# A two-layer graph network on one core: edge keys formed by another engine, copies reordered at a seam, and a branch set elsewhere

## The reference

```
h = relu(layernorm(x))
# layer 0: two graph convolutions; S(h)[d] = sum of h[s] over edges (s, d)
h = relu(relu((h + S(h)) W1 + b1) W2 + b2)
x = x + relu((h + S(h)) W3 + b3) W4 + b4
h = relu(layernorm(x))
# layer 1: message passing
y = mlp3(h; WM, bM)            # per edge source, the same for all edges of a node
x = x + mlp3([h, S(y)]; WU, bU)
```

## Time and profile before

| | |
|---|---|
| median of 3 runs | 923.52 us (922.7 to 924.86) |
| the profiled execution | 923.8 us |
| its span, first to last instruction | 921.9 us |
| PE busy | 862.5 us (94%) |
| DVE busy | 697.5 us (76%) |
| ACT busy | 479.4 us (52%) |
| POOL busy | 395.4 us (43%) |
| DMA | 126.85 MB, mean 138 GB/s |

### The profile page before, as it was taken

One profiled execution on the slowest core, in us unless ns is written; L12 is line 12 of the kernel. 1 busy time (PEld: TensorE's weight loads), 2 busy tenths in 40 slices (PEclk: granted clock), 3 DMA queues, 4 the chain that ended last, 5 costly groups with the idle time before them and its releaser, 6 DMA issues.

```text
span 921.9 us, 25227 instructions
## 1 busy us (share of the span) xinstructions
PE 862.5 (94%) x11291; PEld 710.6 (77%) x11291; DVE 697.5 (76%) x658; ACT 479.4 (52%) x573; POOL 395.4 (43%) x281
## 2 busy tenths in 40 slices
PE   0588999999899999899999999999999999999998
PEld 0367898999898999678877777777778866777776
DVE  7879999999999997385545656654565676787785
ACT  2753646655444454274545555454545555555543
POOL 5888888888000000307645566410110143444532
PEclk9989899999999999999999999999999999999999
DMA  3025255444443244405444344434433567888873
GB/s 112 19 88 156 85 156 157 132 139 130 143 143 122 95 143 143 136 23 160 119 140 121 104 129 127 127 99 134 121 99 86 150 196 204 229 237 244 230 218 107
DMA packets 81856, 126.85 MB, mean 138 GB/s; under 512 B 10160, under 2 KB 58544, under 8 KB 81616
## 3 DMA queue, kind: packets, MB, share of 16 engines
q1 hardware_dynamic: 78608, 121.98, 44.0%
q0 software_dynamic: 3136, 3.22, 1.7%
HBM read 84.22 MB, written 40.94 MB: 136 GB/s over the span
## 4 chain that ended last, share of the span: by engine, by line
PE 55%; ACT 1%; DVE 1%; issue 1%; POOL 0%; POOLq 0%; DVEq 0%; ACTq 0%
PE net_ps_hi L1343 15%; PE net_ps_lo L1343 15%; PE net_ps_lo L1360 7%; PE net_ps_hi L1360 7%; PE net_ps_mt L1288 5%; PE net_ps_ft L1288 2%; PE net_ps_check L1378 1%; PE net_ps_hi L1288 1%; PE net_ps_lo L1288 1%; ACT net_wide L1171 1%; PE net_ps_mt L1390 1%; DVE net_wide L867 1%; PE net_ps_mt L1430 0%; ACT net_hid L1174 0%; PE net_ps_ft L1297 0%
## 5 line engine op out<-in xcount | busy, mean ns | idle before, releaser
L1343 PE MATMUL net_ps_hi<-net_wide,net_first 128*128 128x512 f32 (+2 forms) x637 | 246.7, 390 | 0.0
L1343 PE MATMUL net_ps_lo<-net_wide,net_first 128*128 128x512 f32 (+2 forms) x637 | 238.8, 378 | 0.0
L867 DVE CAST net_wide<-net_raw 128x3584 fp32r<-128x3584 uint8 (+2 forms) x90 | 206.9, 2306 | 41.8 <-PE net_ps_lo L1360 15.8
L1171 ACT ACTIVATE net_wide<-net_raw 128x3584 fp32r<-128x3584 uint8 (+2 forms) x64 | 193.6, 3025 | 79.1 <-PE net_ps_lo L1343 46.3
L607 PE MATMUL build_ps_out<-build_parts_pad,build_cnts 128*128 128x195 bf16 x2401 | 226.7, 254 | 1.0 <-ACT build_cnts L474 1.0
L345 DVE TENSOR_TENSOR build_hot_lo<-build_grid_lo,build_keys_t 128x4096 bf16<-128x4096 bf16 x98 | 220.4, 2281 | 0.0
L607 PEld LDWEIGHTS build_ps_out<-build_parts_pad,build_cnts 128*128 128x128 fp8e4 x2401 | 206.8, 100 | 5.3 <-ACT build_cnts L474 1.1
L474 ACT ACTIVATE build_cnts<-build_ps_cnt 128x980 uint16<-128x980 f32 (+2 forms) x173 | 148.9, 912 | 117.8 <-PE build_ps_cnt L587 115.4
L1343 PEld LDWEIGHTS net_ps_hi<-net_wide,net_first 128*128 128x128 f32 x637 | 119.7, 188 | 28.0 <-issue 7.5
L1343 PEld LDWEIGHTS net_ps_lo<-net_wide,net_first 128*128 128x128 f32 x637 | 119.9, 188 | 23.0 <-issue 2.6
L867 POOL CAST net_wide<-net_raw 128x3584 fp32r<-128x3584 uint8 (+2 forms) x28 | 84.8, 3030 | 109.7 <-PE net_ps_hi L1360 53.1
(11 more groups left out here) (192 smaller groups left out, 712.1 us busy)
## 6 DMA issues: line engine op xcount, KB each, us to landing
net_raw<-edge_counts SPq DMA_DIRECT2D x154, 448.0 KB, 3.7
edge_counts<-build_cnts SPq DMA_DIRECT2D x168, 224.0 KB
net_raw<-edge_counts SPq DMA_DIRECT2D x14, 336.0 KB, 3.3
net_raw<-edge_counts SPq DMA_DIRECT2D x14, 224.0 KB, 2.6
xres<-in_x SPq DMA_DIRECT2D x1, 1568.0 KB, 7.1
out<-xres SPq DMA_DIRECT2D x11, 128.0 KB, 4.2
build_rows<-in_dst_rows,build_row_i POOLq DMA_INDIRECT x49, 3.9
build_edges<-in_edges,build_start_i POOLq DMA_INDIRECT x49, 3.4
```

The source lines that it names most:

```text
L867: return issue(expanded[e % WIDE_RING][:, 0:n, :, :].rearrange("p w a d -> p (w a d)"), raw[e % RAW_RING][:, 0:n, :, :].rearrange("p w a d ...
L1171: expand(act, lambda to, x: nc.scalar.activation(to, x, ACT.Identity), e).then_inc(grown["act"], 1)
L1343: last = nc.tensor.matmul(ps[(b + 1) % 2][:, 0:n * P], first[:, c, lo:lo + H], expanded[e % WIDE_RING][:, 0:n, k, :], start=(c == 0), stop ...
```

## The change

- `find_keys` is gone from VectorE. ScalarE makes four 16-bit planes per pair straight from the gathered edges (`take_bytes`: three instructions of 128 elements; `take_distances`: two of 64), behind its copies of steps 0 and 1 of the pair two ahead of use. TensorE combines them while turning: four products (256, 128, 128, 128 columns) in place of two transposes of 128. The factor 64 is put back by `copy_keys`.
- All groups have 4 windows (the first 2, the last 3). Rows of a group are gathered one group ahead of its edges; from the seventh group on (g >= 6) its rows are compared six pairs ahead and the starts are written five pairs ahead.
- In the written-out beginning, keys of pair 1 are turned and copied right after the first four count steps, those of pair 2 after six.
- The use of pair 0 waits for the features' third parts piece by piece.
- At the seam, ScalarE makes the copy of the high part of y for the last three blocks (`upper_y`), VectorE splits block 12 before it expands its next piece, and ScalarE expands its piece before `upper(11)`.
- SyncE reads the flag and branches two stores earlier; its last two stores and the wait for all stores stand behind the branch.
- The check reads the edges and not the keys.

The core of the diff (line numbers in its headers left out):

```
-SPANS = [(0, 2), (2, 6), (6, 10), (10, 14), (14, 18)] + [(w, min(w + 2 * STEP, NW)) for w in range(18, NW, 2 * STEP)]
+SPANS = [(0, 2)] + [(w, min(w + STEP, NW)) for w in range(2, NW, STEP)]
-ROWS_BEHIND = {2: (4,), 3: (5,), 5: (6, 7), 6: (8,)}
...
-    return {4: (1, 2), 5: (3, 0)}.get(g, (FIRST_PAIR[g] - 6 - 2 * (g - 6), 0))
+    return {4: (2, 1), 5: (4, 1)}.get(g, (FIRST_PAIR[g] - 6, 1))
...
-    return {3: (1, 1), 4: (2, 1), 5: (4, 1)}.get(g, (FIRST_PAIR[g] - 5 - 2 * (g - 6), 1))
+    return {3: (1, 3), 4: (3, 1), 5: (5, 1)}.get(g, (FIRST_PAIR[g] - 5, 1))
...
                 for g in range(2, len(SPANS)):
                     gather_edges(g, *SPANS[g])
-                    for later in ROWS_BEHIND.get(g, ()):
-                        gather_rows(later, *SPANS[later])
+                    if g + 2 < len(SPANS):
+                        gather_rows(g + 2, *SPANS[g + 2])
...
-                def find_keys(g):
-                    lo, hi = SPANS[g]
-                    n = hi - lo
-                    dve.wait_ge(edges_in[g], 16 * n)
-                    src, dst = edges[:, lo:hi, :, 0], edges[:, lo:hi, :, 1]
-                    link(v.tensor_scalar(tile_no[:, 0:n, :], src, 7, None, ALU.logical_shift_right))
-                    v.scalar_tensor_tensor(keys[:, 0, lo:hi, :], tile_no[:, 0:n, :], float(-P), src, ALU.mult, ALU.add)
-                    link(v.scalar_tensor_tensor(scaled[:, 0:n, :], dst, 64.0, tile_no[:, 0:n, :], ALU.mult, ALU.add))
-                    last = v.tensor_tensor(keys[:, 1, lo:hi, :], scaled[:, 0:n, :],
-                                           node64[:, lo:hi, None].broadcast_to([P, n, RUN]), ALU.subtract)
...
+                def take_bytes(u):
+                    g = group_of(u)
+                    to = key_bytes[:, u % BYTE_RING, :, :].rearrange("p k (w e) -> p k w e", e=RUN)
+                    source = edges[:, 2 * u:2 * u + both(u), :, :].bitcast(U8).broadcast_to([P, 2, RUN, 4])
+                    act.wait_ge(edges_in[g], 16 * (SPANS[g][1] - SPANS[g][0]))
+                    nc.scalar.activation(to[:, 0, :, :], source[:, :, :, 0], ACT.Identity, scale=1 / 64)
+                    nc.scalar.activation(to[:, 1, :, :], source[:, :, :, 1], ACT.Identity, scale=-4.0)
+                    nc.scalar.activation(to[:, 2, :, :], source[:, :, :, 0], ACT.Sign, bias=cut[:, 0:1])
+
+                def take_distances(u):
+                    to = key_bytes[:, u % BYTE_RING, 3, :].rearrange("p (w e) -> p w e", e=RUN)
+                    for t in range(2):
+                        w = min(2 * u + t, NW - 1)
+                        last = nc.scalar.activation(to[:, t, :], edges[:, w, :, 1], ACT.Identity, bias=node128[:, w:w + 1],
+                                                    scale=float(-P))
+                    last.then_inc(keyed, 1)
...
                         copy_counts(u, k)
+                        if 0 < u < NU - 2 and k == 0:
+                            take_bytes(u + 2)
+                        if 0 < u < NU - 2 and k == 1:
+                            take_distances(u + 2)
...
                 def turn_keys(u, to):
-                    pe.wait_ge(keyed, group_of(u) + 1)
-                    for k in range(2):
-                        last = nc.tensor.transpose(to[:, k, :], keys[:, k, 2 * u:2 * u + 2, :].rearrange("p w e -> p (w e)"),
-                                                   ident_b[:, :])
-                    return last
+                    pe.wait_ge(keyed, u + 1)
+                    low, tile, top, away = (key_bytes[:, u % BYTE_RING, i, :] for i in range(4))
+                    nc.tensor.matmul(to, top, minus_b[:, None, :].broadcast_to([P, 2, P]), start=True, stop=False)
+                    nc.tensor.matmul(to[:, 0, :], low, ident_b[:, :], start=False, stop=False)
+                    nc.tensor.matmul(to[:, 1, :], tile, ident_b[:, :], start=False, stop=False)
+                    return nc.tensor.matmul(to[:, 1, :], away, ident_b[:, :], start=False, stop=True)
...
+                    if BLOCKS - 1 in at("ty", p - 1):
+                        split_y(BLOCKS - 1)
                     if p + AHEAD < 2 * LATER and EXPAND[p + AHEAD][0] == "dve":
                         grow(p + AHEAD)
...
+                def upper_y(b):
+                    w, n = windows(b), size(b)
+                    act.wait_ge(y_high, b + 1)
+                    nc.scalar.activation(by_turn(second[:, w, 0:F], b), turned_view(high_f, b), ACT.Identity).then_inc(y_upper, 1)
...
-                flagged = flag(sp)
-                for b in range(BLOCKS - 4, BLOCKS):
+                for b in range(BLOCKS - 4, BLOCKS - 2):
                     store(sp, b)
-                general_sync(sp, flagged, stored, 16 * BLOCKS)
-                sp.wait_ge(stored, 16 * BLOCKS)
+                def last_stores():
+                    for b in range(BLOCKS - 2, BLOCKS):
+                        store(sp, b)
+                    sp.wait_ge(stored, 16 * BLOCKS)
+                general_sync(sp, flag(sp), last_stores)
```

145 lines of the change are left out of this document (80 added, 65 removed).

## The result

The changed kernel takes **918.57 us** in the median of six runs (918.34 to 920.29), before it 923.61 (six runs, 922.7 to 924.86): ratio 0.9947, 95% interval 0.9936 to 0.9957. It is 5.0 us faster where 16.5 were forecast, and lies outside the range given. The profiled execution took 918.48 us, its span 916.7.

The account below looks back on a forecast made before the run. It took VectorE and TensorE as both full in build, with key-making extra on VectorE. Gains 9.7 + 6.2 - 1.0 + 2.1 = 17.0, less 0.5, gave 16.5 us off: 907.0 us, eight in ten from 903.5 to 913.0.

Parts of the forecast that it names:

- the rate of a pair: Build after pair 4: TensorE sets the pace at 12.66 us per pair instead of 12.97, gaining 6.2 us.
- rival A: Build: ScalarE brings the keys 0.38 us late in 22 pairs, 8.4 us less gain, 915.4 us; chance 0.10.
- The gathers are as many; per two pairs eight of them, of about 2 us: they keep up.: Build: GpSimd's gathers, eight per 25 us at about 2 us each, were claimed to keep pace.
- Pairs 1 to 3, gain 9.7: Early build: waits and slow-clock stretches vanish, so these pairs take 35.1 us instead of 44.80.
- have long landed: Early build: the wait for edges moves to ScalarE a pair later, when the edges are already there.
- The beginning, loss 1.0: Start: first keys and small ScalarE instructions delay pair 1 by 1.0 us; bounds 2.7 later or 2 earlier.
- The 0.5 kept back for pairs: Build: 0.5 us deducted from the 17.0 us gain for pairs missing the floor by 0.02 us.
- The seam, gain 2.1: Net phase's seam: reordered split, copy and expansions save 2.1 us; bounds 0.3 and 3.5.
- The 1.76: Seam: TensorE's 1.76 us wait ending at 762.04 goes, as block 12's split comes first; gain 1.8.
- the 1.49: Seam: TensorE's 1.49 us wait shrinks, but most returns as a longer wait at 752.10.
- The end, 0: End of kernel: moving SyncE's branch gains nothing, since it lay beside the store's landing; bounds -0.4 to +0.5.
- Rival C: Early build: fifth and sixth groups' comparisons or starts cause a hold and clock dip; 4 to 6 us less, 912; chance 0.15.

Follow-up runs that it names:

- the two runs that took it away: Changed kernel with comparisons and starts from the eighth group on one pair earlier: 913.55 us; changed kernel with one-element VectorE memsets in pairs 17 to 24: 909.23 us.
- memset run: Changed kernel plus a one-element-per-partition memset on VectorE behind the third quarter's match in pairs 17 to 24: 909.23 us, ratio 0.9844.
- the one experiment on it that can be read: Changed kernel with TensorE's and ScalarE's rounding steps of the fifth and sixth sevenths ahead of count steps 5 and 6: 922.0 us, ratio 0.9976.
- seam run: Changed kernel with the seam's old order and VectorE copying y's upper part for all blocks, moved SyncE branch kept: 921.26 us, ratio 0.9974.
- first disturbed run: Changed kernel rerun unaltered while TensorE paused dozens of times with nothing shown to wait for: 950.45 us, ratio 1.023.
- the nine disturbed ones: Changed kernel, unaltered or with one of the follow-up edits, while TensorE paused dozens of times without a shown cause: 946.43 to 959.86 us.
- grouping runs: Kernel before with only the new grouping, VectorE still making keys, run three times: 941.48, 939.89 and 936.49 us; ratios 1.0018, 1.0004, 1.0063.

## Why the prediction was wrong, step by step

- **Direction and the rate of a pair: right.** Pairs 3 to 5, 7, 8, 10, 11, 13 and 15 to 20 take 12.65 to 12.69 us, forecast 12.66. No wait of TensorE for hot_lo behind pair 0. ScalarE's five took 1.17 us and TensorE waited for them only where the edges were late; rival A did not come. The rule of the Trainium skill that stood beside it ("ScalarE: Activation LUTs", "Rules for kernel authors"), which gives adds and multiplies to VectorE, did not bear here, where VectorE was the full engine (50.00 of 50 us).
- **The step that failed: "The gathers are as many; per two pairs eight of them, of about 2 us: they keep up."** The 2 us was read from before, whose gathers were all issued by 228 us and had no wait for starts behind the first. They measured 9.8 to 12.4 us each for six of the last seven, so the last edges landed at 323.3 us and were wanted at 317.65. Cost: 7.0 us in pair 21, shown by the two runs that took it away (913.55, 909.23).
- **Pairs 1 to 3, gain 9.7: too high by 2.8.** They took 98.86 - 60.99 = 37.87 us, forecast 35.1. In pair 1 the turning waited 0.65 us, since ScalarE stood 1.52 us for the edges of pair 3, which were to "have long landed". In pair 2 two things came together, ScalarE's copies without a gap and a pause of TensorE in the middle of a count step:

```profile
64.28 0.31 ACT L429 ACTIVATE build_key_bytes<-edges 128x128 bf16<-128x128 uint8 x1 [1.52 <-DMA edges<-in_edges,build_start_i]
...
71.57 2.75 ACT L469 ACTIVATE build_cnts<-build_ps_cnt 128x980 uint16<-128x980 f32 x3 [2.34 <-PE build_ps_cnt L595]
```

```profile
73.98 1.00 PE L595 MATMUL build_ps_cnt<-build_hot_a,build_hot_lo 64*128 64x49 bf16 x66 [1.01 <-issue]
```

  From pair 2 on the first third of the use stands behind count steps 0 to 2, and steps 5 and 6 of pair 1 stand just ahead of them, so five count steps follow each other where the two pairs meet. TensorE needs 0.56 us for one (three in 1.68) and a copy takes 0.88. VectorE's hot_lo, for which TensorE had waited before 69.49 and 71.60, is in time now, but ScalarE's pace stood behind it. The memset run shows it alone: there steps 1 and 2 of pair 2 begin 0.82 and 0.88 us after the one before, and the pair takes 13.36 us, 0.7 more than 12.66. The pause before 73.98 is not ScalarE's: all that the step waits for was done, the trace names nothing, and with the same copies it is 0.19 us in the memset run. Pairs 1 and 2 cost 1.7 us less there (10.15 and 13.36 for 10.80 and 14.42): 0.65 is the wait for edges, absent there, and 0.8 the shorter pause.
- **The beginning, loss 1.0: was 1.9.** It lay within the bounds given (2.7 later). Of it 0.75 stood at the first count already (28.70 for 27.95). What in the chain costs the rest stays open; the one experiment on it that can be read made it worse (64.98).
- **The 0.5 kept back for pairs: was 1.8**, most of it in pairs 6, 9 and 14, 0.3 to 0.65 us each, for which the trace names nothing.
- **The seam, gain 2.1: 2.2** by the traces, 2.5 by the run without it. The 1.76 went as forecast. Of the 1.49, most was to come back before the piece at 752.10; that pause grew from 0.27 to 0.63 only, and the new 0.21 and 0.37 ate about as much, so that the sum came right in part by luck. **The end, 0: 0.1** by the tail of the trace (from the start of TensorE's last product to the end 3.70 us before, 3.57 after), which is no more than the scatter: with the same branch the tail is 3.49 in the seam run and 3.70 in the memset run.

Added up: 7.0 + 2.8 + 0.9 + 1.3 = 12.0 us of missing gain, against 16.5 - 5.0 = 11.5 measured; the small gains of seam, end and pair 23 are the difference. Rival C had the right kind (a group's data late, a clock dip behind it) and its price of 4 to 6 us, 912 us, but for the fifth and sixth groups' comparisons or starts, and with a chance of 0.15. The range reached up to 913.0 and held only one such hold.

## What to carry to other kernels

A duration read from before belongs to the neighbours and the schedule that it had there: where a change moves transfers in time or takes away instructions beside which they ran, ask what else their duration hung on. When the leading engine gets faster, list every transfer that is issued by pace of another engine and set its landing time, at its worst duration, against the new date of use; the last group has no later work to hide behind. An experiment that moves the suspected transfer together with what it waits for, and one that changes only what lets it in, gave both the cause of the pause and a kernel 1.6% faster than before.

## What the runs showed of the hardware that was not expected

- GpSimd's indirect gathers (128 rows) took 0.95 us with VectorE idle (at 254.09 in the first disturbed run), 1.9 to 3.1 us between back-to-back matches of 2.28 and 3.48 us, and at other times 9.8 to 12.4 us, when only the reduction or `find_starts` lets one in. Behind a one-element memset of 0.06 us it was over. What starts it is open: it began only behind a wait of GpSimd of 5.7 us or more, but not behind every such wait; in the changed code it came at the same gather, the 92nd of 98, in all six undisturbed executions, whatever the time (237 to 251 us) and VectorE's distance: there it is the first behind such a wait (7.79 to 10.0 us). In the nine disturbed ones it stood behind a wait of 15.35 us or more and was quick. In the grouping runs a gather at 64.5 us even took 18.4 us (in two of three).
- TensorE's pauses with nothing to wait for go with times of 950 us and more for the kernel that took 918.6 at another time, and of 926 to 967 in single runs of the kernel before, which took 923.6; what causes them no run shows; one chip was quiet in one set of runs and disturbed in a later one. In the disturbed sets with both kernels the changed one was not faster (1.013, 1.023). The gain of 0.5% holds for quiet runs alone; why the changed kernel suffers more was not tried.
